# Maxima of the FFN's gated rows over 1024 columns in two pieces, in place of 512 columns in four

## The reference

```python
def _act_quant(x):
    scale = 127.0 / jnp.clip(jnp.max(jnp.abs(x), axis=-1, keepdims=True), 1e-05)
    xq = jnp.clip(jnp.round(x * scale), -128.0, 127.0) / scale
    ...
h = jax.nn.silu(_bitlinear(x, W1))      # 2048 numbers for each row
return _bitlinear(h, W2)                # quantises h by its own row maximum first
...
x = x + _L0_xattn_ref(_layernorm(x, axis=-1), ctx_2048, ctx_2048)
x = x + _L0_ffn_ref(_layernorm(x, axis=-1), L0_ffn_W1, L0_ffn_W2)
```

## Time and profile before

| what | kernel before |
|---|---|
| median of three runs | 781.38 us |
| the profiled execution | 782.53 us |
| its span, first to last instruction | 780.7 us |
| around the span | 1.8 us |
| mean granted PE clock, of full speed | 0.987 |
| PE busy | 718.7 us (92%) |
| DVE busy | 693.9 us (89%) |
| ACT busy | 634.8 us (81%) |
| POOL busy | 630.5 us (81%) |

### The profile page before, as it was taken

The page is one execution under the profiler, slowest core; times in us unless marked ns, Lnnn a source line. Parts: engine busy times, 40 slices in busy tenths (PEclk is TensorE's granted clock), DMA queues, the critical chain, the costliest instruction groups (busy, mean ns, idle before and its releaser), DMA issues.

```text
span 780.7 us, 13868 instructions
## 1 busy us (share of the span) xinstructions
PE 718.7 (92%) x4324; PEld 280.2 (36%) x4324; DVE 693.9 (89%) x1588; ACT 634.8 (81%) x1017; POOL 630.5 (81%) x627
## 2 busy tenths in 40 slices
PE   0578699999999999999999999999999999999984
PEld 0112243333444444333344444333334344433322
DVE  2779999999999999999999999999999999997552
ACT  5486788888888898888888889888888888888852
POOL 3764778888889888888888998888888889877761
PEclk9999699999999999999999999999999999999998
DMA  8673213444333443344433334333443334330100
GB/s 293 167 197 111 55 43 107 109 110 109 98 92 84 109 99 78 96 109 109 109 101 92 85 105 100 81 92 109 110 109 103 94 86 101 82 82 25 46 28 13
DMA packets 53960, 76.66 MB, mean 98 GB/s; under 512 B 7808, under 2 KB 32384, under 8 KB 52864
## 3 DMA queue, kind: packets, MB, share of 16 engines
q1 hardware_dynamic: 53888, 75.79, 37.0%
HBM read 41.94 MB, written 8.39 MB: 64 GB/s over the span
## 4 chain that ended last, share of the span: by engine, by line
PE 83%; DVE 8%; DMA 3%; issue 2%; ACT 2%; SPq 1%; POOL 1%; POOLq 0%; ACTq 0%; DVEq 0%
PE pv L912 15%; PE mxp L902 15%; PE st L892 14%; PE bank_b L943 14%; PE dn L921 7%; PE bank_a L972 7%; PE bank_b L972 7%; DVE mx L727 4%; PE bank_a L931 3%; DMA late<-w 1%; DMA qs<-ql 1%; DMA qs<-qh 1%; ACT probs L585 1%; DVE late L796 1%; PE bank_a L954 1%
## 5 line engine op out<-in xcount | busy, mean ns | idle before, releaser
L585 ACT ACTIVATE probs<-st,sm 128x512 f32<-128x512 f32 x512 | 336.6, 687 | 52.7 <-PE st L892 26.9
L503 POOL TENSOR_TENSOR sums<-probs 128x512 f32<-128x512 f32 x256 | 333.3, 1321 | 20.8 <-ACT probs L585 20.8
L727 DVE TENSOR_REDUCE mx<-mxp 128x1 f32<-128x512 f32 x512 | 332.8, 676 | 18.5 <-PE mxp L902 14.9
L902 PE MATMUL mxp<-ks,qs 96*128 96x512 f16 x512 | 191.0, 403 | 18.2 <-DVE mx L727 12.4
L892 PE MATMUL st<-qs,ks 98*128 98x512 f16 x512 | 200.8, 394 | 1.7 <-ACT probs L585 1.6
L943 PE MATMUL bank_b<-w2t,late 128*128 128x512 f16 x512 | 128.1, 383 | 3.0 <-ACT late L615 3.0
L912 PE MATMUL pv<-probs,vt 128*32 128x512 f32 x1024 | 124.0, 602 | 0.0
L495 POOL TENSOR_TENSOR ql<-xn,qh 128x512 f16<-128x512 f32 x32 | 37.2, 1164 | 67.2 <-ACT qh L606 67.2
L892 PEld LDWEIGHTS st<-qs,ks 98*128 98x128 f16 x512 | 52.8, 103 | 99.3 <-ACT probs L585 40.1
L902 PEld LDWEIGHTS mxp<-ks,qs 96*128 96x128 f16 x512 | 50.7, 99 | 103.3 <-DVE mx L727 78.6
L801 DVE TENSOR_REDUCE hmx<-late 128x1 f32<-128x512 f32 x128 | 84.3, 679 | 1.1
(11 more groups left out here) (79 smaller groups left out, 896.6 us busy)
## 6 DMA issues: line engine op xcount, KB each, us to landing
cs<-ctx SPq DMA_DIRECT2D x32, 256.0 KB, 4.2
xs<-x SPq DMA_DIRECT2D x32, 256.0 KB, 4.0
late<-w SPq DMA_DIRECT2D x8, 1024.0 KB, 9.2
ks<-kh SPq DMA_DIRECT2D x64, 128.0 KB, 3.2
qs<-qh SPq DMA_DIRECT2D x64, 128.0 KB, 3.6
xr<-x SPq DMA_DIRECT2D x32, 256.0 KB, 3.0
vt<-values_t SPq DMA_DIRECT2D x32, 256.0 KB, 2.9
out<-late SPq DMA_DIRECT2D x32, 256.0 KB, 2.0
```

The lines of the kernel that those rows point to most:

```text
L503: pool.tensor_tensor(sums[:, pair, h, :], probs[:, 2 * pair, h, :], probs[:, 2 * pair + 1, h, :], ALU.add).then_inc(sum_done, 1)
L585: act.activation(probs[:, c, h, :], st[u % 2][:, :], ACT.Exp, scale=sm1[:, r, ESC:ESC + 1]).then_inc(exp_done, 1)
L727: dve.reduce_max(mx[:, slot.ring(off), NC * h + c:NC * h + c + 1], mxp[m % 2][:, :], axis=AX.X).then_inc(max_done, 1)
L902: pe.matmul(mxp[m % 2][:, :], qs[0:3 * DH, r, h, c * P:(c + 1) * P], ks[0:3 * DH, r, h, :], start=True, stop=True).then_inc(mx_done, 1)
```

## The change

Three things change together. `hidden_max` is done twice for each tile, over 1024 columns of the gated row each time (pieces 0 and 1, then 2 and 3), in place of four times over 512. The first stands in unit 15, behind gate 2, and the second in unit 1, behind gate 3 and ahead of `invert`. The tile `hmx` has two columns for each tile in place of four, so that `hidden_scale` reduces two numbers and waits for two parts. The places that fall away are the one in unit 13 between gate 0 and gate 1 and the one in unit 0 behind gate 3. The order of everything else on every engine stays.

```diff
-    hidden_max=[29, 31, 32, 33],
+    hidden_max=[31, 33],
...
-        hmx = sb("hmx", [P, RING, FC], f32)
+        hmx = sb("hmx", [P, RING, 2], f32)
...
-            def hidden_max(slot, off, fc):
-                wait(dve, gate_done, slot, FC, off, fc + 1)
-                dve.tensor_reduce(out=hmx[:, slot.ring(off), fc:fc + 1], in_=hu[:, fc * D:(fc + 1) * D], axis=AX.X, op=ALU.max,
+            def hidden_max(slot, off, n):
+                wait(dve, gate_done, slot, FC, off, 2 * n + 2)
+                dve.tensor_reduce(out=hmx[:, slot.ring(off), n:n + 1], in_=hu[:, 2 * n * D:2 * (n + 1) * D], axis=AX.X, op=ALU.max,
                                   apply_absolute_value=True).then_inc(hidden_parts, 1)
...
-                wait(dve, hidden_parts, slot, 4, off, 4)
+                wait(dve, hidden_parts, slot, 2, off, 2)
```

## The result

| | before | after |
|---|---|---|
| median of seven runs | 783.85 us | 788.47 us |
| lowest and highest | 780.64, 785.32 | 787.36, 790.21 |
| ratio after / before | | 1.0083 (1.0065 to 1.0101) |
| the profiled execution's span | 780.7 us | 788.4 us |
| DVE busy | 693.9 us (89%) | 689.2 us (87%) |

A forecast was written before the change was run, and what follows sets the result against it. PE was taken to set the lap, with DVE's lateness reaching it through the row maxima: 27 x 0.22 = 5.9 us, plus 0.5 (last tile) and 0.2 (three laps before), sum 6.6; 781.38 + 6.6 = 788.0 us, range 780.8 to 791.3.

The forecast's parts named there:

- low bound: Lower bound for the 1024-column reduction on DVE: 0.665 ns a column, pitch 0.94 us; nothing reaches PE, 781.4 us.
- Steps 1 to 5: DVE from gate 0 to the transposition: fewer, longer reductions in new places make the transposition 0.39 us late.
- step 1: Between gates 0 and 1: removing the reduction gains only 0.23 of 0.60 us, since gate 1 waits for its tanh.
- Step 6: Smaller edits change nothing countable; factor and consumers move up to 0.39 us, hidden; if uncovered, up to 0.1 us more.
- Step 7: At `attend` on DVE: its existing wait takes 0.08 us of the delay, leaving 0.31 for the three row maxima.
- Step 8: On PE: maxima matmul moves to 432.44, `second` to 432.66, behind DVE instead of the copy; 0.22 us late each lap.
- The last tile: Only DVE latency counts there: L808 starts at 766.68 in place of 766.16, 0.5 us later.
- A: Rival, faster: gate 1 sets PE, and its coming 0.23 us earlier gains 6.2 us, giving 775.2 us; chance 0.06.
- B: Rival: DVE is the bound and gives back what it saves, 0.10 us a lap, giving 778.7 us; chance 0.05.
- V: Rival theory of the experiments: DVE's amount of work sets the lap; reducing one piece should be at least 3% faster.
- C: Rival, no change: the delay stays hidden, under 0.17 us at the transposition; 781.4 to 782 us; chance 0.17.

The follow-up runs named there:

- the run with one piece: Kernel before with only piece 3's 512-column reduction kept, behind gate 3, the maxima of pieces 0, 1 and 2 left out: ratio 0.9963, laps of 21.607 us.
- the kernel that fills the hole: Kernel before with both pairs merged, one unit 14 row maximum moved between gates 0 and 1, first merged reduction ahead of gate 2: ratio 0.9981, laps of 21.640 us.
- places: Kernel before with its four 512-column reductions unmerged but moved to the change's places, two behind gate 2, two behind gate 3: ratio 1.0079, laps of 21.846 us.

## Why the prediction was right

- *What bounds the kernel.* Right. DVE's amount of work does not set the lap; its lateness from gate 0 to the row maxima behind `attend` does, when it is more than the cover. That is shown by the run with one piece (49.9 us of work taken away bring 0.02 us a lap) and by the spare work in unit 10 (work added there costs nothing). That PE sets the lap otherwise is argued from its share of the chain (83%) and of the laps, of whose 584.3 us it is recorded busy for 580.9; no run took work from PE. In the same stretch DVE is busy for 564.3 us, 97%, and is still not the bound.
- *The new reduction.* 1.14 us of pitch and 1.226 of duration were forecast from the 128- and the 512-column rows; they are 1.13 and 1.22. The low bound of 0.94 was never near. The rule of the Trainium skill (VectorE: DVE Perf Modes, "The perf-mode tier table") that tensor_reduce has only the 1x form agrees with the trace: the 512 columns more cost 537 ns (1216 ns in the mean against 679), 1.05 ns for a column, and not the 0.665 of the low bound.
- *Steps 1 to 5.* Gate 1 1.10 us behind gate 0 (measured 1.09), gate 3 4.62 (4.61), the wait for gate 3 0.73 (0.72), the transposition 0.39 late (0.37). That the empty place at gate 1 matters (step 1) is shown by the kernel that fills the hole.
- *Step 6.* The factor's delay is hidden, as forecast: ACT's wait for it (L621 for L827) grew from 16.8 to 29.7 us in total, and PE doesn't see it: with the spare work ahead of the factor or behind it, `second` is late by what the row maxima are late (0.26 and 0.39 us) less 0.08 to 0.09 for the copy.
- *Step 7* took 0.11 us (0.12 up to the next row maximum) and not 0.08: `attend` stands 10.18 us behind gate 0 after, 9.92 before, so 0.26 is left of 0.37.
- *Step 8 was wrong in its mechanism, and right only in sum.* I expected PE to lose 0.22 us, all of it at `second`. It loses 0.16 there (`second` is 12.33 us behind gate 0, 12.18 before by the rounded starts, 12.17 by the unrounded ones). The other 0.07 are lost at the maxima matmul at 439.84, which I had put at nothing, taking PE's waits from `second` on to be round trips that only move with PE. Together 0.23 for 0.22. That the two agree is partly luck: a transposition 0.02 less late and 0.03 more taken up by `attend` make up for a cover of the copy that was counted at 0.09 and leaves 0.02 to 0.03. With a delay laid behind `attend` nothing makes up for it, and 0.38 comes in place of 0.30.
- *The sum.* 5.9 us were forecast for the laps; 5.8 came in one pair of traces and 5.6 in the other. 27 x 0.23 is 6.2, but one lap of the kernel before takes 21.98 us, 0.35 more than the others, for an idle time ahead of gate 0 that the changed kernel doesn't have:

```profile
440.98 0.74 DVE L721 SCALAR_TENSOR_TENSOR kl<-cs,sm,kh 128x512 f16<-128x512 f32 x1
442.24 0.69 DVE L796 SCALAR_TENSOR_TENSOR late<-late,bank_b 128x512 f32<-128x512 f32 x1 [0.52 <-ACT late L640]
```

These two rows are of the kernel before. The chain there puts 0.40 us down to "issue". The same 0.52 us stand in the same lap of the second execution and of `places`, and three laps earlier in all three kernels with spare work, so they are no accident of one execution; their cause is open. In `places`, where gate 1 has idle time ahead of it, the lap is 0.02 us longer by them, and in the others 0.35.
- *The last tile.* For the way from gate 0 to L808 0.5 us were forecast; it is 6.24 us in place of 5.77. But what follows the last like lap grew by only 0.1 and 0.3 us, since the transposition's 0.37 us of lateness at its beginning is hardly handed on: the last gate 0 stands 73.9 us behind it in place of 74.2. That there are fewer row maxima behind it is the likely reason, and not shown. The estimate of 0.7 for the whole tail was too much by half or more.
- *The rivals.* A fell: piece 3 starts 2.05 us behind gate 0 after and 2.06 before, so the 8.1 us of waits were no stall of PE. B fell with V: a lap got longer and not 0.1 us shorter. The rule of the Trainium skill (Perfetto Trace Analysis, "Optimizing Scalar/DVE Operations") is not met in its condition, a saturated engine, though its some 60 ns for an instruction are the right size for what is saved: a merged pair has a pitch of 1.13 us in place of 1.19. C is what the run with only the later pair merged shows: a delay under the cover costs nothing.

The time forecast was 788.0 us and the median is 788.47, but that closeness is partly luck. The forecast stood on the 781.38 us of three runs of the kernel before, and the median of seven is 783.85. In differences, 6.6 us were forecast (0.84%); the ratio measured is 1.0083, the medians are 4.6 us apart, and by the traces the edit's part is 5.9 us (0.75%): 7.7 less 1.8 of the start in one pair, 6.0 less 0.1 in the other.

## What to carry to other kernels

A hole in an engine's list is only worth its removal if what follows can start; look up what the next instruction waits for before counting the gain (here 0.23 of 0.60 us), and what the moved work now stands in front of. Where an engine is nearly full but does not set the time, its total is no guide: the same 0.38 us cost between nothing and 0.38 us a lap, depending on the place. Follow a delay past the first wait that it reaches, since the next double-buffered wait can take a second bite.

## What was not expected of the hardware

The laps are more regular than the time: 21.85 to 21.86 us in the two executions of the changed kernel, while the start varied by 4.6 us over the traces with the row "transposition of the second tile", more than most of the effects measured here. Most of the spread of the whole times (780.6 to 785.3 us for the kernel before) may come from there; that was not measured. For an effect inside the laps the lap is the sharper measure.
